# Four graph-attention layers in one kernel: in layer 0 a third set of exponentials, scores issued ahead of sums and values, q's rows in three half buffers, all stages written out

## What is computed

```
q, k, v = h @ Wq.T + bq, h @ Wk.T + bk, h @ Wv.T + bv      # 4 heads of 32
scores  = clip(q . k / sqrt(32), -10, 10); scores = -10 where adj == 0
attn    = softmax of scores over each chunk of 128 nodes    # 8 chunks, each normed by itself
ctx     = sum over the chunks of attn_chunk @ v_chunk
out     = layernorm(ctx @ Wo.T + bo + h) * gamma + beta
x       = x + out
```

## Time and profile before

| | |
|---|---|
| time, median of 3 runs | 1999.77 us (1999.49 to 2002.91) |
| the profiled execution | 1999.09 us, span of the core 1997.2 us |
| busy over the whole span | PE 1644.5 us (82%), DVE 1601.0 (80%), ACT 1338.3 (67%), POOL 134.9 (7%) |
| layer 0's exponentials | first starts at 48.3 us, the last at 630.8 us |
| instructions | 36885 |

### The profile page before, as it was taken

One profiled execution on the slowest core, in us unless ns is written; L12 is line 12 of the kernel. 1 busy time (PEld: TensorE's weight loads), 2 busy tenths in 40 slices (PEclk: granted clock), 3 DMA queues, 4 the chain that ended last, 5 costly groups with the idle time before them and its releaser, 6 DMA issues. The chain is left out here.

```text
span 1997.2 us, 36885 instructions
## 1 busy us (share of the span) xinstructions
PE 1644.5 (82%) x13620; PEld 1053.7 (53%) x13620; DVE 1601.0 (80%) x2710; ACT 1338.3 (67%) x1751; POOL 134.9 (7%) x131
## 2 busy tenths in 40 slices
PE   3988888898886677999999768876787668999997
PEld 1444443444433456777777556665665454455454
DVE  3888998998898457888889889898989866766764
ACT  2776576676664476777776888888988825545543
POOL 1001111111010000000000000000000000000000
PEclk9999999999998588999999878888988879999999
DMA  8645635635622311111111121122123200000000
GB/s 230 157 110 127 138 94 119 148 89 128 144 72 72 121 43 43 44 43 42 42 48 49 53 68 65 65 65 65 65 80 97 96 23 1 11 22 11 11 11 21
DMA packets 74923, 146.50 MB, mean 73 GB/s; under 512 B 11937, under 2 KB 34722, under 8 KB 74754
## 3 DMA queue, kind: packets, MB, share of 16 engines
q1 hardware_dynamic: 74754, 144.23, 26.3%
HBM read 101.85 MB, written 8.78 MB: 55 GB/s over the span
## 5 line engine op out<-in xcount | busy, mean ns | idle before, releaser
L1241 ACT ACTIVATE g<-s_all,steep_d 128x1024 fp8e4<-128x1024 f32 x608 | 642.3, 1135 | 38.8 <-DMA s_all<-s_rows 21.6
L600 ACT ACTIVATE e<-s_ps 128x1024 f32<-128x1024 f32 x256 | 248.3, 1023 | 23.0 <-PE s_ps L450 18.4
L1325 DVE TENSOR_TENSOR g<-g,edge 128x1024 int32<-128x1024 int32 x192 | 227.9, 1220 | 31.8 <-ACT g L1241 31.7
L1176 PE MATMUL acc<-arena,g 128*128 128x102 bf16 (+1 forms) x3072 | 209.5, 229 | 17.8 <-DVE sums L1332 14.1
L1176 PEld LDWEIGHTS acc<-arena,g 128*128 128x128 fp8e4 x3072 | 201.2, 100 | 35.5 <-issue 27.2
L760 DVE SCALAR_TENSOR_TENSOR e<-e,bound 128x1024 f32<-128x1024 f32 x160 | 191.2, 1229 | 32.5 <-ACT e L600 32.2
L1176 PE MATMUL acc<-parts,g 128*128 128x102 bf16 (+1 forms) x3072 | 208.6, 228 | 6.3 <-DVE sums L1332 6.3
L1176 PEld LDWEIGHTS acc<-parts,g 128*128 128x128 fp8e4 x3072 | 200.3, 99 | 21.5 <-issue 13.0
L446 PE MATMUL s_ps<-qs,ks 128*128 128x512 f32 x512 | 194.6, 490 | 7.0 <-DMA ks<-split 5.4
L462 PE MATMUL sum_ps<-e,pick 128*32 128x256 f32 x2048 | 139.3, 390 | 67.0 <-DVE e L760 60.0
L2031 ACT ACTIVATE z<-z,shift 128x1024 f32<-128x1024 f32 x64 | 73.5, 1149 | 169.4 <-DVE shift L2099 169.4
(11 more groups left out here) (189 smaller groups left out, 2417.2 us busy)
## 6 DMA issues: line engine op xcount, KB each, us to landing
s_all<-s_rows SPq DMA_DIRECT2D x96, 512.0 KB, 3.7
inv_all<-inv_rows SPq DMA_DIRECT2D x256, 128.0 KB, 2.9
qs<-split SPq DMA_DIRECT2D x128, 128.0 KB, 3.2
ks<-split SPq DMA_DIRECT2D x128, 128.0 KB, 3.2
x<-in_x SPq DMA_DIRECT2D x8, 512.0 KB, 6.6
inv_rows<-inv SPq DMA_DIRECT2D x32, 128.0 KB, 1.7
adj_in<-in_adj SPq DMA_DIRECT2D x8, 512.0 KB, 4.3
out_x<-x SPq DMA_DIRECT2D x8, 512.0 KB, 3.2
```

The costliest lines, as they stand in the source:

```text
L600: act.activation(e[:, 2 * (i % 2) + hp, :, :], s_ps[:, hp, :, :], ACT.Exp, scale=SCALE).then_inc(exp_done, 1)
L1176: ins = pe.matmul(self.acc[:, bank, o:o + self.NS], self.g[:, h % RING, jt, it * P:(it + 1) * P], self.upper[par][:, jt, h, :, :].rearrang ...
L1241: act.activation(self.g[:, h % RING, jt, :], self.s_all[:, h % 2, :], ACT.Relu, bias=self.steep_d[par][:, jt, h:h + 1], scale=STEEP, satur ...
L1325: dve.tensor_tensor(both, both, c.edge[:, some, :].rearrange("p t n -> p (t n)").bitcast(I32), ALU.bitwise_and).then_inc(self.g_ready, 1)
```

## The change

In words:

- `e` gets 6 tiles in place of 4: three sets of two pairs. A step uses the set `(16 * b + i) % 3` (`e_of`).
- On PE the scores of `i+1` are issued ahead of the sums and values of `i-1`, no longer behind them. Projection work stays at the end of the step.
- `pv_done` starts at 3 in place of 2. The wait of `exps` keeps its number, so it now asks for the values of `i-3`. The wait of `copy_chunk` is raised by one, so it asks for the same as before.
- q's stacked rows: in place of two whole buffers one tile `qs` of three halves. Batch `n` uses the halves `2n % 3` and `(2n+1) % 3`. Where these are 2 and 0 (`swapped`), the two projection matmuls write their halves of `aux` in the other order, so that a stepped slice fits. Each stacking DMA is now written as two rows of 512 a partition. SP waits, ahead of `stack_q_hi(n)`, until the scores of the first half of batch `n-1` are done.
- `residual(b - 1, ..., 1)` moves on DVE from step 10 to step 11.
- `walk_through` takes the place of `walk` in layer 0: all 8 stages are written out, without a loop.

```diff
+def walk_through(eng, prepare, stage, tail):
+    prepare(0, 0)
+    for b in range(B):
+        stage(b, b % 2, b == 0, b < B - 1)
+    tail()
...
-        qs = [sb(f"qs{i}", [P, H, N], F32R) for i in range(2)]
+        qs = sb("qs", [P, 3, H, HALF], F32R)
...
-        e = sb("e", [P, 4, 2, HALF])
+        e = sb("e", [P, 6, 2, HALF])
...
+        def e_of(b, i, hp):
+            return e[:, 2 * ((STEPS * b + i) % 3) + hp, :, :]
+        def swapped(n):
+            return (2 * n) % 3 == 2
...
             def stack_q_hi(n, par):
-                stack(n, qs[par], 0, (0, 1), q_hi, q_hi_stacked)
+                if n > 0:
+                    wait_apart(c, sp, s_ready, 32 * n + 48)
+                stack(n, q_rows(n), 0, (0, 1), q_hi, q_hi_stacked)
...
             def q(n):
                 pe.wait_ge(nm.h_t_ready, nm.upto(n))
-                project_rows(pe, aux, wq[:, :], c.h_t).then_inc(q_projected, 1)
+                for i in range(2):
+                    at = 1 - i if swapped(n) else i
+                    ins = pe.matmul(aux[:, at * HALF:(at + 1) * HALF], wq[:, :], c.h_t[:, i * HALF:(i + 1) * HALF],
+                                    start=True, stop=True)
+                ins.then_inc(q_projected, 1)
...
                 for i in range(STEPS):
                     before = (b, par, i - 1) if i >= 1 else (b - 1, 1 - par, STEPS - 1)
                     after = (b, par, i + 1) if i + 1 < STEPS else (n, 1 - par, 0)
-                    if not (first and i == 0):
-                        sums(before[0], before[2])
-                        values(*before)
                     if more or i + 1 < STEPS:
                         if i + 1 == STEPS:
                             stacks(n)
                         for hp in range(2):
                             scores(*after, hp)
+                    if first and i == 0:
+                        pe.wait_ge(v_ready, b + 1)
+                    else:
+                        sums(before[0], before[2])
+                        values(*before)
...
             def copy_chunk(b, i):
-                act.wait_ge(pv_done, 16 * b + i + 3)
+                act.wait_ge(pv_done, 16 * b + i + 4)
                 act.wait_ge(pair_weighed, 8 * b + i // 2 + 1)
...
-            act.sem_inc(pv_done, 2)
-            walk(act, prepare, stage, tail)
+            act.sem_inc(pv_done, 3)
+            walk_through(act, prepare, stage, tail)
...
-                        elif i == 10:
+                        elif i == 11:
                             residual(b - 1, 1 - par, 1, True)
```

More of the change, by code:

```diff
@@ L213, in layer0 @@
         w_add, a_add = v[1][:, 0:2, :], v[1][:, 2:6, :]
-        e = sb("e", [P, 4, 2, HALF])
+        e = sb("e", [P, 6, 2, HALF])
         adj_in = [chunk[:, :, :].rearrange("p (t a) n -> p t (a n)", t=4).bitcast(I32),
-                  e[:, :, :, :].rearrange("p t a n -> p t (a n)").bitcast(I32)]
+                  e[:, 0:4, :, :].rearrange("p t a n -> p t (a n)").bitcast(I32)]
         inv = sb("inv", [P, QUARTER])
@@ L295, in stack, with q_rows, k_rows @@
                     for h in range(H):
-                        sp.dma_start(dst[copy * DH:(copy + 1) * DH, h, :].bitcast(F32),
-                                     split[h * DH:(h + 1) * DH, part, :].bitcast(F32)).then_inc(stacked, 16)
+                        sp.dma_start(dst(copy, h).bitcast(F32),
+                                     split[h * DH:(h + 1) * DH, part, :].rearrange(
+                                         "p (a n) -> p a n", a=2).bitcast(F32)).then_inc(stacked, 16)
+            def q_rows(n):
+                first = (2 * n) % 3
+                halves = slice(0, 3, 2) if swapped(n) else slice(first, first + 2)
+                return lambda copy, h: qs[copy * DH:(copy + 1) * DH, halves, h, :]
+            def k_rows(par):
+                return lambda copy, h: ks[par][copy * DH:(copy + 1) * DH, h, :].rearrange("p (a n) -> p a n", a=2)
             def stack_q_hi(n, par):
-                stack(n, qs[par], 0, (0, 1), q_hi, q_hi_stacked)
+                if n > 0:
+                    wait_apart(c, sp, s_ready, 32 * n + 48)
+                stack(n, q_rows(n), 0, (0, 1), q_hi, q_hi_stacked)
             def stack_q_lo(n, par):
-                stack(n, qs[par], 1, (2, 3), q_split, q_lo_stacked)
+                stack(n, q_rows(n), 1, (2, 3), q_split, q_lo_stacked)
             def stack_k_hi(n, par):
-                stack(n, ks[par], 0, (0, 2), k_hi, k_hi_stacked)
+                stack(n, k_rows(par), 0, (0, 2), k_hi, k_hi_stacked)
             def stack_k_lo(n, par):
-                stack(n, ks[par], 1, (1, 3), k_split, k_lo_stacked)
+                stack(n, k_rows(par), 1, (1, 3), k_split, k_lo_stacked)
             def prepare(n, par):
@@ L356, in tail @@
                 inverses(B - 1, 1, 1)
-            walk(sp, prepare, stage, tail)
+            walk_through(sp, prepare, stage, tail)
         @block.gpsimd
@@ L407, in tail @@
                 rstd_out(B - 1, 1)
-            walk(pool, prepare, stage, tail)
+            walk_through(pool, prepare, stage, tail)
         @block.tensor
@@ L446, in scores @@
                     ins = pe.matmul(s_ps[:, hp, j, :], ks[par][:, 2 * hp + j, jt * P:(jt + 1) * P],
-                                    qs[par][:, 2 * hp + j, half * HALF:(half + 1) * HALF], start=True,
+                                    qs[:, (2 * b + half) % 3, 2 * hp + j, :], start=True,
                                     stop=jt not in MASKED)
@@ L462, in sums @@
                         ins = pe.matmul(sum_ps[h * DH:(h + 1) * DH, :], pick[:, at:at + DH],
-                                        e[:, 2 * (i % 2) + h // 2, h % 2, q * QUARTER:(q + 1) * QUARTER],
+                                        e_of(b, i, h // 2)[:, h % 2, q * QUARTER:(q + 1) * QUARTER],
                                         start=(jt % GROUP == 0 and q == 0), stop=(jt % GROUP == GROUP - 1 and q == 1),
@@ L471, in values @@
                     ins = pe.matmul(ctx_ps[h * DH:(h + 1) * DH, :], v[par][:, i % T, h * DH:(h + 1) * DH],
-                                    e[:, 2 * (i % 2) + h // 2, h % 2, :], start=True, stop=True,
+                                    e_of(b, i, h // 2)[:, h % 2, :], start=True, stop=True,
                                     tile_position=(0, h * DH))
@@ L499, in stage @@
                         scores(b, par, 0, hp)
-                    pe.wait_ge(v_ready, b + 1)
                 for i in range(STEPS):
@@ L542, in tail @@
                 output(B - 1, 1)
-            walk(pe, prepare, stage, tail)
+            walk_through(pe, prepare, stage, tail)
         @block.scalar
@@ L599, in exps @@
                     act.wait_ge(pv_done, 16 * b + i + 1)
-                act.activation(e[:, 2 * (i % 2) + hp, :, :], s_ps[:, hp, :, :], ACT.Exp,
+                act.activation(e_of(b, i, hp), s_ps[:, hp, :, :], ACT.Exp,
                                scale=SCALE).then_inc(exp_done, 1)
             def copy_chunk(b, i):
-                act.wait_ge(pv_done, 16 * b + i + 3)
+                act.wait_ge(pv_done, 16 * b + i + 4)
                 act.wait_ge(pair_weighed, 8 * b + i // 2 + 1)
@@ L754, in clip @@
                 dve.wait_ge(exp_done, 32 * b + 2 * i + hp + 3)
-                tile = e[:, 2 * (i % 2) + hp, :, :]
+                tile = e_of(b, i, hp)
                 if jt in MASKED:
@@ L882, in tail @@
                 update(B - 1, 1)
-            walk(dve, prepare, stage, tail)
+            walk_through(dve, prepare, stage, tail)
 class Shared:
```

## The result

The changed kernel takes **2127.56 us** (median of 4 runs, 2122.65 to 2132.85), the kernel before 1999.74 (4 runs). The ratio is 1.0636, with a 95% interval from 1.0607 to 1.0664: 128 us slower. The prediction was 2101 us, range 2070 to 2150, slower with a chance of 0.91. All ratios and intervals leave out one launch, of the twelve of experiment 3, that took 2040.12 us at a lower granted clock (0.825 in place of some 0.92); the median given there is of all twelve.

What follows compares the result with a forecast made beforehand. DVE was taken to bound the kernel, PE close behind. Ring laps of 675.8 us plus 7 us for output projections and slow first scores gave layer 0 683 us, 101 more than before: 2101 us, range 2070 to 2150.

Steps and rivals of the forecast that it cites:

- What bounds the kernel before: Layer 0: DVE fullest (66.1 of 73 us), PE close behind; smoother work could take at most 60 us of waits.
- The ring: Layer 0: values, copy, exponentials, scores, then next values, one lap a step without slack; 2101 us, chance 0.86.
- The question that the prediction left open: ACT's queue: whether exponentials could pass the waiting copy, which no row of the profile could show.
- The lap: One turn of the ring in layer 0: 5.17 us, masked 5.57; 79 and 48 of them make 675.8 us.
- The projections: PE, end of step: only the output projection shows, 7 times 0.6 us and 8 times 0.2, together 5.8 us.
- DVE, SP and the loop: DVE's moved `residual`, SP's q copies and writing out the stages: nothing; SP's bound 28 us.
- The clock: PE's clock in layer 0: higher level taken throughout, as the new pauses are 1.7 and 0.4 us, never 3.8.
- the swinging clock: Rival: the ring, with one step in four at half rate, 32 x 2.1 = 67 us more: 2168 us, chance 0.05.
- Both cases of my list: The rivals of the ring setting the pace (2101 us, 0.86) and the ring with swinging clock (2168 us, 0.05).
- The row: Profile before, PE: after a gap of 3.81 us four scores took 2.08 us, against 1.21 after short gaps.
- The range: Whole kernel: 2070 to 2150 us; upwards 25 us for slower hand-overs and 28 for SP's bound, all of both unlikely.
- Faster: Rival: exponentials run ahead in layer 0 and DVE's 60 us of waits go: 1940 us, chance 0.06.

Runs made afterwards that it cites:

- experiment 3: The changed kernel with PE's old order put back (sums and values of i-1 ahead of scores of i+1): 2000.82 us, 0.9997 of the kernel before.
- experiment 1: The changed kernel with ACT's copy of step i-2 moved behind both exponentials of step i: 1961.86 us, 0.9813 of the kernel before.
- experiment 4: The kernel before with PE's new order and `residual` at step 11 alone (two sets, whole q buffers, hardware loop): 2137.97 us, 1.0686 of before.
- experiment 6: The changed kernel with the copy behind both exponentials, but exponentials waiting for the values of i-2 again: 2053.53 us, 1.0266 of the kernel before.
- experiment 5: The kernel before with PE's new order, `residual` at step 11 and layer 0's stages written out: 2119.85 us, 1.0607 of before.
- experiment 7: The changed kernel with 12 matmuls of zeros behind the values of every odd step, filling PE's pause: 2097.53 us, 1.0490 of the kernel before.

## Why the prediction was right, and where its sum was short

- **What bounds the kernel before** was right: DVE, with PE close behind, and at most some 60 us to win in waits. Experiment 1 won 38 of them, with DVE then busy for 96% of a stage.
- **The ring** was right as described: the exponentials queue behind a copy that waits for values which the change put behind the scores. Experiments 1, 4 and 6 show its three parts: take the copy out of the front and it is gone, the PE order alone makes it, and a wait of the exponentials for the same values makes a shorter one. The question that the prediction left open is answered too: ACT never passed the waiting copy. On its timeline of the changed kernel copies and pairs of exponentials alternate throughout, and no exponential starts ahead of the copy of i-2.
- **The lap** was priced at 5.17 and 5.57 us and measured 5.14 and 5.61. Copy to exponential took 0.49 us (323.26 - 322.77), not 0.63; the end of the exponentials to the start of the sums took 0.71 (318.12 + 1.94 to 320.77), not 0.61, and sums to copy 2.00, not 1.99; a masked lap cost 0.47 more, not 0.40. The errors nearly cancel, which is luck: 79 x 5.14 + 48 x 5.61 = 675.3 us, against 675.8.
- **The projections** were right in kind: only the output projection shows, 0.39 us at step 10 in place of 0.6, and nothing at step 14: 7 x 0.39 = 2.7 us, where the sum held 5.8.
- **DVE, SP and the loop** at nothing: shown together by experiment 3 for the old order. In the new order SP's and q's part held too (experiment 5 beside the changed kernel; the moved `residual` stands in both and was not tried there alone), but the loop is worth some 9 us there. My reason for nothing, that its cost falls on engines that wait, was wrong for a ring: every hand-over in it counts. It cost nothing here only because the change takes the loop out.
- **The clock** is the term that was mis-sized. I took the higher level throughout, since no pause of the new laps comes near 3.8 us, and gave the swinging clock a chance of 0.05. It swings. The sum held 1 us for slow scores at the start; the 19 slow laps are 30.7 us longer than their like at full clock, and experiment 7 gave back 28 in the layer. That is the 25 us by which the layer (708.2 us) is longer than the 683 forecast; with the pauses filled it takes 680.3. Both cases of my list were thus true together: the ring sets the pace, and on top of it 19 laps in 127 are slow, at 1.4 to 1.7 us each, where I had priced one in four at 2.1. The row alone could not have told me: in the trace before, each of the six stretches with a granted clock of 0.50 after layer 0's start lies at a pause of PE of 3.2 to 3.8 us; in the changed one none after the start lies at a pause over 1.64. The page of the Trainium skill that I had weighed against the row ("TensorE: Matmul & The Clock Gate", section "A second HAM failure mode: psum-queue depth-cycling") tells of another kernel, in which short pauses between groups of matmuls made the clock swing; this trace agrees with it, with pauses of 1.63 us and a granted clock of 0.50 in 19 laps. My reading of one long gap as the only thing that lowers the clock was wrong.
- **The range** held 2127.6 partly by luck. Its upper half was room for slower hand-overs (25 us) and for SP's copies (28 us), and neither came; the clock, which used that room, had no place in it.
- **Faster** did not come, and experiment 1 shows on what it hung: 1962 us, where that rival was priced at 1940 with all of DVE's waits gone.

## What to carry to other kernels

When an engine's order is changed or a buffer added, follow one lap through every engine's list: a wait that is relaxed in one instruction does nothing if the instruction ahead of it in the same queue still waits for the same event. An idle engine's long wait (here ACT's copy, 156 us at no cost) is the first thing to look at when work is moved behind the event it waits for. And a new order with the copy left in front lost 6.4%, with the copy behind it won 1.9%, while the other parts of the change won nothing without it (experiment 3): one part of such a change can't be judged with the others missing.

## What the runs showed of the hardware

- The granted clock of PE fell to 1.2 GHz in layer 0 (after its start) without any pause over 1.64 us near it. It came at the same two steps of nearly every stage.
